# The last batch's projection and norm move into the first experts' units, and the first half is routed earlier

## The reference, cut to what matters

```python
# mixing: h_t = A*h_{t-1} + B x_t along the sequence, y = W h + b
x = _layernorm(x + _L0_attn_ref(x, A, B, W, b))
# cross attention: q from x, k and v from the context, rotary embedding,
# scores where |i-j| <= 50 only, softmax, values, output projection Wo
x = _layernorm(x + _L0_xattn_ref(x, ctx, ctx, Wq, bq, Wk, bk, Wv, bv, Wo, bo))
# experts
router_logits = silu(x @ router_w1) @ router_w2
expert_probs = softmax(router_logits.transpose(0, 2, 1), axis=-1)   # over tokens
expert_weights, token_indices = top_k(expert_probs, 64)
expert_weights = expert_weights / (expert_weights.sum(-1) + 1e-09)
expert_inputs = x[token_indices]
gate, value = silu(expert_inputs @ w1), expert_inputs @ w2
expert_out = (gate * value) @ w3
output = scatter_add(expert_out * expert_weights)
x = _layernorm(x + output)
```

## Time and profile before

| what | value |
|---|---|
| median of 3 runs | 1098.94 us |
| the profiled execution, whole | 1104.09 us |
| its span, first to last instruction | 1102.3 us |
| PE, DVE, ACT, POOL busy | 91%, 66%, 54%, 63% |
| mean granted TensorE clock | 0.964 of full speed |

### The profile page before, as it was taken

The page is one execution under the profiler, slowest core; times in us unless marked ns, Lnnn a source line. Parts: engine busy times, 40 slices in busy tenths (PEclk is TensorE's granted clock), DMA queues, the critical chain, the costliest instruction groups (busy, mean ns, idle before and its releaser), DMA issues.

```text
span 1102.3 us, 21835 instructions
## 1 busy us (share of the span) xinstructions
PE 1001.6 (91%) x6436; PEld 847.6 (77%) x6436; DVE 728.9 (66%) x2174; ACT 590.7 (54%) x1226; POOL 690.6 (63%) x785
## 2 busy tenths in 40 slices
PE   4799999999999998848999999999999999999990
PEld 3577777777777776526888788888888888888890
DVE  4678888787778776835678465646557674855634
ACT  1155555555555556525756465655556566655541
POOL 5556666666666665246466677676767767677644
PEclk8899999999999999867999999999999999999995
DMA  6343443333333432416567466656686665666646
GB/s 186 85 105 93 102 102 98 101 99 100 99 98 99 105 80 68 146 36 225 136 134 177 106 157 135 176 117 169 139 228 163 135 176 114 175 134 158 156 82 177
DMA packets 114992, 142.44 MB, mean 129 GB/s; under 512 B 15184, under 2 KB 88144, under 8 KB 114768
## 3 DMA queue, kind: packets, MB, share of 16 engines
q1 hardware_dynamic: 87600, 106.62, 33.1%
q0 software_dynamic: 24576, 33.57, 17.8%
q10 hardware_dynamic: 2720, 1.17, 0.4%
HBM read 90.71 MB, written 29.36 MB: 109 GB/s over the span
## 4 chain that ended last, share of the span: by engine, by line
PE 50%; DMA 2%; DVE 1%; ACT 1%; POOL 1%; issue 1%; SPq 0%; DVEq 0%; POOLq 0%; ACTq 0%
PE y_bank L1272 16%; PE gate_bank L1272 16%; PE value_bank L1272 16%; PE turn_bank L1282 2%; DMA acc_rows<-y,slots_now 1%; DMA last<-acc_rows 1%; DVE stats L1448 0%; DMA rw<-in_rw 0%; PE y_bank L1325 0%; DVE w_lo L1423 0%; DVE last L1459 0%; POOL acc_rows L1232 0%; POOL rw_placed L1251 0%; ACT w_hi L1349 0%; ACT gate L1362 0%
## 5 line engine op out<-in xcount | busy, mean ns | idle before, releaser
L1232 POOL DMA_INDIRECT acc_rows<-y,slots_now x128 | 202.7, 1584 | 129.9 <-ACT y L1376 101.2
L1441 DVE TENSOR_TENSOR hidden<-gate,value_bank 128x512 f32<-128x512 f32 x128 | 88.0, 687 | 196.5 <-ACT gate L1362 191.4
L916 DVE CUSTOM_DVE_ANT_0 scored<-score,band 128x178 f32<-128x178 f32 x512 | 150.1, 337 | 72.3 <-PE score L577 65.6
L765 ACT ACTIVATE probsT<-scoreT 128x356 f32<-128x356 f32 x256 | 117.5, 468 | 141.3 <-PE scoreT L606 109.9
L1362 ACT ACTIVATE gate<-gate_bank 128x512 f32<-128x512 f32 x128 | 76.6, 599 | 157.6 <-PE value_bank L1272 152.1
L1272 PE MATMUL y_bank<-w_hi,h_hi 128*128 128x256 f32 x512 | 147.5, 288 | 2.7 <-DVE weight_of L153 2.7
L1272 PE MATMUL y_bank<-w_lo,h_hi 128*128 128x256 f32 x512 | 143.3, 280 | 0.0
L1272 PE MATMUL y_bank<-w_hi,h_lo 128*128 128x256 f32 x512 | 143.2, 280 | 0.0
L1423 DVE TENSOR_TENSOR w_lo<-arena,w_hi 128x1024 fp32r<-128x1024 f32 x96 | 117.6, 1226 | 26.0 <-ACT w_hi L1349 22.3
L577 PE MATMUL score<-k_stack,q_stack 96*128 96x178 f32 x512 | 122.8, 323 | 8.9 <-DVE nmax L916 6.1
L577 PEld LDWEIGHTS score<-k_stack,q_stack 96*128 96x128 f32 x512 | 87.5, 192 | 38.9 <-DVE nmax L916 21.7
(11 more groups left out here) (177 smaller groups left out, 2406.9 us busy)
## 6 DMA issues: line engine op xcount, KB each, us to landing
arena<-in_w SPq DMA_DIRECT2D x96, 512.0 KB
k_stack<-high_k SPq DMA_DIRECT2D x128, 64.0 KB, 2.3
q_stack<-high_q SPq DMA_DIRECT2D x128, 64.0 KB, 2.3
arena<-in_xT SPq DMA_DIRECT2D x16, 256.0 KB, 2.9
arena<-in_x SPq DMA_DIRECT2D x16, 256.0 KB, 3.1
arena<-in_cT SPq DMA_DIRECT2D x16, 256.0 KB, 3.6
k_stack<-low_k SPq DMA_DIRECT2D x64, 64.0 KB, 2.3
q_stack<-low_q SPq DMA_DIRECT2D x64, 64.0 KB, 2.3
```

Source lines behind the costliest of these rows:

```text
L765: nc.scalar.activation(probsT[g % 2][:, u % HG, :, :].rearrange("p a s -> p (a s)"), scoreT[u % 2][:, 0:2 * SPAN], ACT.Exp, scale=1.0 / DH ...
L916: op = nc.vector.tensor_tensor_reduce(scored[t % 2][:, q, :], score[t % 2][:, q * SPAN:(q + 1) * SPAN], band[:, q, :], -1.0, BIG, ALU.add, ...
L1232: nc.gpsimd.indirect_dma_start(dram["acc"][c], bass.IndirectOffsetOnAxis(ap=now[:, m:m + 1], axis=0), y[m][:], None, compute_op=ALU.add).t ...
L1441: nc.vector.tensor_tensor(hidden[f % 2][:], gate[f % 2][:], value_bank[f % 2][:], ALU.mult).then_inc(hidden_ready, 1)
```

## The change

1. In every step, `invert_sums` of the first pair moves on ACT from slot 4 to slot 6 (in step 16 it stays in slot 4).
2. The first half's router moves: silu to step 10, logits to step 11 slot 13, exponential and scaling to step 12 slots 1 and 2, the eight rounds to steps 12 to 15 (two each), `weigh_picked` to step 15 slot 7, its transpositions to slot 10, `place_picked` to slot 12.
3. POOL gathers expert 0's rows in step 15, ahead of that step's `inverse_sums(-1)`. PE transposes them in step 16 slot 5, DVE makes both parts of them in slot 6.
4. ACT and DVE split expert 0's w1 and w2 in steps 15 and 16, into buffers that share room with batch 14's `q_stack` and `k_stack`. SP loads them ahead of the four copies into `acc`.
5. Step 17 is gone. Step 16 does batch 14's O, norm, OX and R in earlier slots. Of batch 15, the last denominators are inverted at the beginning of `experts`; O and statistics are done in unit 0, the estimate after unit 1, POOL's refinement and the normalisation in unit 2, OX ahead of unit 3's `up`, R behind its `turn`.
6. The second half's router moves four units later, to units 4 to 10, and its copies into `acc` to unit 3.
7. The loop over steps makes two turns, and steps 10 to 16 are written out; units 0 to 11 are written out, and the loop over units in the first half makes one turn.

```diff
+        NORMAL = {"O": (4, 7), "statistics": 8, "estimate": 9, "normalise": 11, "OX": 13, "x2T": 14, "R": 15, "r1": 15}
+        DRAIN = {"O": (1, 2), "statistics": 2, "estimate": 3, "normalise": 5, "OX": 6, "x2T": 7, "R": 8, "r1": 9}
 ... SP, end of mixing
-            sp.wait_ge(x2_kept, 16 * (NB // 2) + 1)
-            (four copies x2 -> acc); step(Iter(0, 15, 4))
             sp.wait_ge(ready["U"], NB); sp.wait_ge(ready["V"], NB); sp.wait_ge(xb_ready, NB)
             for n, name in enumerate(("w1", "w2", "w3")):
                 sp.dma_start(keep["raw"][n], ...)
+            sp.wait_ge(x2_kept, 16 * (NB // 2) + 1)
+            (four copies x2 -> acc)
-            for i in (16, 17):
+            for i in (15, 16):
                 step(Iter(0, i, 4))
-            sp.wait_ge(x2_kept, 16 * NB + 1)
 ... POOL, step(it)
+                drain = it.fixed and it.i >= NB
+                if drain and there(it, "O"):
+                    inverse_deviation(it, "O")
                 if behind:
                     inverse_sums(it, -2)
-                if there(it, "O"):
+                if there(it, "O") and not drain:
                     inverse_deviation(it, "O")
                 if there(it, "Y"):
                     inverse_deviation(it, "Y")
-                if behind:
+                if it.fixed and it.i == NB - 1:
+                    pool.wait_ge(route.placed, 1)
+                    (rows_now, four indirect gathers)
+                if behind and not drain:
                     inverse_sums(it, -1)
 ... PE, step(it)
+                    if only(it, 11, t, 13):
+                        pe.wait_ge(silu_done, 1)
+                        pe.wait_ge(freed["V"], uses(it, "V"))
+                        (logits, into bank("R"))
+                    if only(it, NB - 1, t, 10):
+                        pe.wait_ge(route.picked, 1)
+                        (two transpositions)
+                    if only(it, NB, t, 5):
+                        pe.wait_ge(rows_in[0], 16 * CB)
+                        pe.wait_ge(scored_ready, NH * NB)
+                        (eight transpositions of rows)
+                        if it.fixed and it.i == 11:
+                            pe.wait_ge(logits_kept, 1)
 ... ACT, step(it)
-                    if t in (4, 12):
-                        invert_sums(it, (t - 20) // 8)
+                    ends = it.fixed and it.i == NB
+                    first = 4 if ends else 6
+                    if t == first or t == 12 and not ends:
+                        invert_sums(it, -2 if t == first else -1)
+                    for n in range(2):
+                        if only(it, NB - 1, t, 10 + 4 * n):
+                            act.wait_ge(scoreT_ready, NH * (NB - 1))
+                            nc.scalar.copy(keep["w_hi0"][n], keep["raw"][n])
 ... DVE, step(it)
+                    for n, (i, at) in enumerate(((12, 7), (12, 14), (13, 1), (13, 14), (14, 1), (14, 14), (15, 1), (15, 4))):
+                        if only(it, i, t, at):
+                            take_eight(dve, route, n)
+                    for n, (i, at) in enumerate(((NB - 1, 13), (NB, 0))):
+                        (w_lo0[n] = raw[n] - w_hi0[n])
 ... experts; LATE = 4
+                if it.is_unit(2):                      # SP
+                    sp.wait_ge(x2_ready, NB)
+                    (store of x2cur)
+                if it.is_unit(LATE - 1):               # PE, ahead of up
+                    turn_x2(it)                        # waits for y_scaled of the unit before
                 up(it)
                 turn(it.step(1))
+                if it.is_unit(0):
+                    project_O()
+                if it.is_unit(1):
+                    pe.wait_ge(freed["O"], NB)
+                if it.is_unit(LATE - 1):
+                    route_x2()
+                    pe.wait_ge(freed["R"], NB + FREED_EARLY)
-                if it.is_unit(0):
+                if it.is_unit(LATE):
                     (logits of the second half)
+                    pe.wait_ge(logits_kept, 1)
                 down(it.step(-1))
+            gather(Unit(0, 1, 0))                      # POOL, ahead of unit 0
+            inverse_sums()
+            invert_sums()                              # ACT, ahead of unit 0
+            add_odd()                                  # DVE, ahead of unit 0
```

More of the change, by code:

```diff
@@ L229, in mixing @@
         probsT = [sb(f"probsT{n}", HG, 2, SPAN) for n in range(2)]
[L230 to L238, removed]
+        sums, rough, inverse, vals, mixed = ([sb(f"{name}0", S), keep[f"{name}1"]]
+                                             for name in ("sums", "rough", "inverse", "vals", "mixed"))
+        attnT = [sb("attnT0", NPAIR, S), keep["attnT1"]]
+        sums_log, halves, x2cur, x2T = keep["sums_log"], keep["halves"], keep["x2cur"], keep["x2T"]
         GB, CB = NB // 2, NC2 // 2
@@ L532, in _ @@
                 step(Iter(0, i, 4))
-            with pool.Fori(0, 3) as j:
+            with pool.Fori(0, 2) as j:
                 for r in (2, 3, 4, 5):
@@ L856, in step @@
                         heighten(FIRST_KEYS, 0)
-                    if t == 9 and there(it, "O"):
+                    if t == slot(it)["estimate"] and there(it, "O"):
                         estimate(it, "O")
@@ L873, in step @@
                         estimate(it, "Y")
-                    if t == 15 and there(it, "R"):
+                    if t == slot(it)["r1"] and there(it, "R"):
                         act.wait_ge(ready["R"], uses(it, "R"))
@@ L958, in step @@
                     maxima(it, t)
-                    if t in (3, 11) and has(it, group(t, 15)):
+                    if t in (3, 11) and has(it, group(t, 15)) and not only(it, NB, t, 11):
                         p = group(t, 15) // 2
@@ L977, in step @@
                         rotated(it, 1)
-                    if t == 8 and there(it, "O"):
+                    if t == slot(it)["statistics"] and there(it, "O"):
                         dve.wait_ge(x1_biased, it.lin(1, -1))
@@ L987, in step @@
                         op.then_inc(freed["U"], 1)
-                    if t == 11 and there(it, "O"):
+                    if t == slot(it)["normalise"] and there(it, "O"):
                         dve.wait_ge(x2_kept, it.lin(16, -31))
@@ L1338, in unit @@
                     down(it.step(-1))
-            turn(Unit(0, 0, 0))
             all_units(pe, unit)
@@ L1389, in unit @@
                 gate_of(it, 2)
+                if it.is_unit(LATE - 1):
+                    act.wait_ge(ready["OX"], NB)
+                    nc.scalar.copy(x2T[:].rearrange("p k s -> p (k s)"), y_bank[0][:]).then_inc(freed["OX"], 1)
                 h_high(it, 1)
@@ L1397, in unit @@
                     columns(it.step(1))
+                if it.is_unit(LATE - 1):
+                    act.wait_ge(ready["R"], NB)
+                    nc.scalar.copy(r1[:, B * S:NB * S], y_bank[1][:, 0:S]).then_inc(freed["R"], 1)
                 if it.at_least(1):
@@ L1501, in unit @@
                         normalise(2 * n + 1)
-            split(Unit(0, 0, 0), 0)
-            split(Unit(0, 0, 0), 1)
-            columns(Unit(0, 0, 0))
+            add_odd()
             all_units(dve, unit)
```

285 lines of the change are left out of this document (201 added, 84 removed).

## The result

The kernel after took 1093.0 us in the median of five runs (1090.3 to 1093.8) against 1098.94 of the kernel before; the ratio is 0.9929 [0.9908, 0.995]. The forecast was 1081.0: a gain, but one of 5.9 in place of 17.9 us, and outside both ranges that were stated (1074 to 1087, and 1071 to 1091). The profiled execution of after took 1093.0 as well, with a span of 1091.1; the one of before was 1104.09 with 1102.3. So the two traces that are compared here lie 11.2 us apart, and the medians 5.9.

The account below looks back on a forecast made before the run. PE, busy 91% of the span, was taken as the bound, with waits in the loop and a poor seam. 8.0 + 0.6 - 7.1 + 22.3 - 5.9 = 17.9 us off 1098.94 gave 1081.0, range 1074 to 1087 (wider: 1071 to 1091).

Parts of the forecast that it names:

- Parts 1 and 2: Loop over steps: logs in slot 6 end PE's 0.64 us wait per step, gain 8.0; one loop turn less, gain 0.6.
- Part 3: First half's router work in steps 10 to 14: a loss of 7.1 us, bounds 4.2 and 13.2.
- The silu with its table loads only moves, from step 14 to 10: nothing: Router on ACT: moving the silu between these steps was put at no cost.
- The upper bound of 13.2: Router in steps 10 to 14: loss if no round is covered and 1.0 us of logit copies and maxima, with scaling, counts.
- rival B: DVE bounds steps 11 to 14: router loss 13.2 instead of 7.1 us, so 1087.1; chance 0.10.
- Part 4: Steps 15, 16 and the seam to the experts: 67.2 us become 44.9, gain 22.3, bounds 14 and 28.
- PE has no long wait: Sign for the trace after: in step 15 PE was to have no long wait.
- the meeting: Meeting of the engines before unit 0's first expert product, put at 2.24 us in the seam's chain.
- rival C: Clock stays high over the seam; chain and start of unit 0's `up` together save 4 us, so 1077; chance 0.06.
- Part 5: Last batch's work inside PE's full expert units: loss of 5.9 us, 2.9 of it products, the rest waits; bounds 2.9 and 10.
- In units 0 and 1 nothing waits: Experts' first units: POOL's last inversion, 6 + 3 us after the meeting, was covered by `up` of 11 us or more.
- in units 1 to 5 for weights or rows: Sign of being wrong: PE waiting in these expert units for weights or rows.

Follow-up runs that it names:

- the part alone: Kernel before with only the logarithm and exponential of the first pair's sums moved on ACT from slot 4 to 6: 1094.41 against 1103.68 us, ratio 0.9925.
- with the rounds moved: Kernel after with the six rounds of eight of steps 12 to 14 in slots 3, 5, 1, 3, 1, 3: 1090.64 us, 0.9914 of the kernel before.

## Why the forecast was wrong, step by step

Held to the two traces, where the sum said 17.9 and 11.2 are seen:

- *Parts 1 and 2: right.* 8.6 were forecast. The step of the loop is 0.74 shorter, not 0.64, and the part alone gave 8.3 us. The wait before OX stayed at 0.85, as argued from DVE's own pause. In the two traces both parts come to some 9.8: a lead of 6.2 at the R of step 9, four more steps of 0.74, and 0.6 for the turn.
- *Part 3: the router, 7.1 forecast, some 9.1 measured* (what steps 10 to 14 take above 26.10 each). Step 11 took 4.0 us more than the loop's step (forecast about 4), steps 12 and 13 0.7 and 0.8 (at most 1.5). The failed step is "The silu with its table loads only moves, from step 14 to 10: nothing". Step 10 paid 2.25 us for it (28.35 less 26.10), and step 14 didn't give it back: a wait of 1.96 for x2cur and two of 0.45 and 0.57 for nmax, all for DVE, took the place of the 2.18 for ACT, and the clock fell to 0.94. So it took 27.44 with no silu in it, where before took 26.10 with it. (The upper bound of 13.2, and with it rival B, adds up to 12.9 from its own terms.)
- *Part 4: the seam, 22.3 forecast; 19.3 measured* to the first product, where the forecast counted to (67.2 less 47.9). By the pieces of its chain, placing ended 2 us late, behind the wait of 2.06 and the slow products in step 15, of which the forecast said "PE has no long wait" (with the rounds moved, where such waits are 0.45 and 1.41 and the clock stays at 1.00, placing ended 19.2 us after the R of step 14; the forecast had 19.6). The four gathers took 0.4 us more than forecast. The wait of O for attnT, named at about 5, was 6.60. From these sums to the last gather of values went 15.5 us, not 13.2, with waits of 0.64, 1.19 and 1.43 in it; only the meeting was cheaper for PE, 0.50 in place of 2.24. From the R of step 14 to the turn of unit 1 it is 22.1, and that this is near 22.3 is luck: `up` of unit 0 came back at the full clock and took 11.0 in place of 13.8 us, which is the start that rival C had, without its high clock in step 16. Four gathers ahead of the sums was a cost of the change and no need of it: the other order gave 6 us.
- *Part 5: the experts, 5.9 forecast, 11.5 measured. This is the step that failed.* The products were put at 2.9, as half of 5.75 "at about half clock", but O's row of 2.56 had a clock of 0.77: at full clock they take 1.89, 0.63 and 1.03, some 3.5. The waits failed more. R's copy: 1.9 (forecast 1.7), but with a stretch at half clock behind it, 4.5 for that unit in place of 2.7. Logits: "PE now waits for DVE's copy of the logits at once: 0.7" was nearly so (0.52), but nothing was said of the weights that POOL sets out for them in the same unit, behind a memset and four gathers: 2.65 of waiting and 1.5 of slow logits, 8.2 for the unit in place of 4.3. "In units 0 and 1 nothing waits": the splits before unit 1 were late by 1.74, and by the forecast's own sign (a wait "in units 1 to 5 for weights or rows") it was wrong. The placing gave 1.6 back, by a fall of the clock that this execution did not have.
- *The base.* The sum was made in an execution of 1104.09 and its difference taken from 1098.94. After's level did not follow before's down: 5 of the 12 us between 1081.0 and 1093.0.

The wait of 1.74 was looked at in the trace alone. POOL's inversion in unit 0 beside DVE's splits of the weights (first POOL and DVE there, then the same split in unit 3):

```profile
487.75 1.80 POOL L1318 TENSOR_TENSOR inverse<-sums,rough 128x256 f32<-128x256 f32 x1
487.30 1.65 DVE L1542 TENSOR_TENSOR w_lo<-arena,w_hi 128x1024 fp32r<-128x1024 f32 x1 [0.25 <-ACT w_hi L1452]
560.42 1.23 DVE L1542 TENSOR_TENSOR w_lo<-arena,w_hi 128x1024 fp32r<-128x1024 f32 x1 [0.24 <-ACT w_hi L1452]
```

The operation that took 0.73 on POOL in step 16 takes 1.80 here, the split 1.65 for 1.23, three of them in a row (1.65, 1.41, 1.71), and `xT_lo` comes behind them. This agrees in kind with the Trainium skill, "SBUF — State Buffer", section "Who interferes with whom", by which a DVE instruction with two SBUF inputs contends with a GpSimd instruction that reads SBUF. The forecast named that rule for the gathers and left it out for unit 0. But the three splits are only 1.1 us longer together than three of 1.23, so they can't be the whole of the 1.74; what the rest is, and whether the wait goes when POOL's work is moved, was not tested. The wait was 1.4 to 1.8 in every trace of after and its variants.

## What to carry to other kernels

Work put into a stretch where the bounding engine is full costs its length plus every wait that it brings, and on PE a wait of about two microseconds can cost nearly twice its length, since the clock may drop behind it (1.89 of waiting, 1.6 for the clock): before moving such work, list for each of its operands who makes it, and behind what. When a step is moved on an in-order engine, ask of each instruction that it overtakes who waits for that one; here four gathers went ahead of four short operations, and PE stood 6.6 us. Ask the same of the DMA engines: large transfers moved into a step stand beside the small ones that it waits for. And take a forecast from an execution whose level is known: one profile 5 us above the median is a term of the sum.

## What the runs showed of the hardware

Waits of 1.9 to 2.7 us in a stretch with PE otherwise full were followed, in some executions, by a stretch of products at the lower of the two clock levels (in the one above, weight loads of 0.33 in place of 0.19 us for 3.4 us). It was so in eight executions of nine behind 1.89, in four of nine behind 2.65, and in none of four behind 0.91. A fall mostly cost 1.4 to 1.7 us (the most were about 2 in the kernel with the silu in slot 3 and 3.0 in the second trace of before), and the same wait of 2.73 had it in one execution and not in another. I had priced waits at their length. It also explains part of the scatter of these kernels: a unit with such a wait differs by 1.7 us between two executions of after (20.53 and 22.27), the units without one by about 0.3 at most between executions.

A gather on POOL took 0.94 to 0.95 us with DVE at rest and 1.66 to 1.90 beside DVE's splits (2.25 in the kernel with the sums first), and POOL's 128x256 operation on two inputs 0.73 and 1.80.
